# Gated tiles on ScalarE, the selection in one piece on VectorE, the second gather in other banks, W2 in quarters

## The chip, the cores and the metric

One Trainium2 chip, one core. A core has TensorE (matmuls into eight PSUM banks), VectorE, ScalarE, GpSimd and SyncE, and 16 DMA engines that all queues share. The metric is the time of one launch in device microseconds; lower is better.

## The reference

The input x is (16, 1024, 512), 16 batches of 1024 tokens. Two residual steps follow each other: a gated cross attention over 64 context tokens a batch (the first half of the kernel, which the change does not touch), and a gated expert step, which it does. The expert step, cut to what matters:

```python
x = x + jnp.tanh(g_ffn[0]) * ffn(_layernorm(x))
# ffn: DM, NEXPERTS, SETS, ESIZE = 512, 32, 4, 32  -> 128 experts of width 32
grouped = x.reshape(b, s // g, g, d)                            # groups of g = 32 tokens
logits = einsum('bntd,des->bntes', grouped, Wc) + bc + tie
perm = (logits == max(logits, over the 32 tokens of a group))   # each expert picks a token of each group
permuted = einsum('bntd,bntes->bnesd', grouped, perm)           # gather
inner = relu(einsum('bnesd,esdf->bnesf', permuted, W1) + b1)
result_permuted = einsum('bnesf,esdf->bnesd', inner, W2) + b2
result = einsum('bnesd,bntes->bntd', result_permuted, perm)     # scatter back
```

W1 and W2 are 8 MB each in float32; every batch needs both whole.

## The kernel before, in words

`experts` writes one instruction stream for each engine by hand; semaphores (`Mark`, with `at(i, k)` for the k-th event of batch i) order them. The loop runs over i = 0 to 16: step i works on batch i, finishes batch i-1, and prepares batch i+1. On TensorE a step is:

1. `gather(i, n)`, n = 0 to 7: selected tokens of one quarter of D (c) and one half of the tokens (h) are multiplied by the one-hot `sel` into banks 4 to 7. ScalarE and VectorE share the copy out to `gat` (`copy`, L1259 and L1302). Each gather waits until both copies of the one before are done. `bias(i)` (L1371) starts the accumulators, banks 0 to 3, and stands behind gather 0. `inner(i, p)` (L1388) multiplies `gat` by one eighth of W1 and runs two gathers behind.
2. `scatter(i-1, t)` (L1426), t = 0 to 7, into banks 4 to 7 in turn; `finish(i-1, t)` (L1306, VectorE) multiplies the tile by the gate into SBUF, and GpSimd adds it to `out` in DRAM with an accumulating DMA (`add_to_out`, L1221). A scatter from the fifth on waits for the finish four back.
3. `outer(i, u)`, u = 0 to 7 (L1406 and L1411): eight parts of W2, in two bank groups in turn. `rest(i, u)` copies each out, one half on ScalarE (L1269), one on VectorE (L1316). `outer(u)` waits for the copies of `outer(u-2)`, and `outer(1)` for the last finish, since it uses banks 4 to 7.
4. `chosen_T(i+1, h)` (L216) transposes the next batch's one-hot matrix, `chosen` (ScalarE, L221) copies it into `sel`.

VectorE also turns `res` in place (`swap`, L1296, eight a step, one behind each gather copy), and makes the selection of the next batch, `pick` (L199, L207, L210: add bias, maximum of the group, compare) for two halves h. The logits of a half are first scaled on GpSimd (`scaled`, L191), and the tokens of the next batch are normalised there (`normed`, L184).

Where the weights lie: three eighths of W1 and five of W2 (u = 0 to 4) stay in SBUF. The others come anew each batch. W1's come in quarters of 256 KB from SyncE (L1159, L1167). W2's u = 5, 6, 7 (`W2_MOVED`) come into the space of `gat` as three DMAs of 1 MB from ScalarE (`load_second`, L1147), once `inner` has read `gat` for the last time. SyncE also loads the next batch's eight token tiles (`load_x`, L174, 256 KB each) and per half two transfers of 256 KB for the logits (L178 and L179). Token tiles 4 to 7 take the places of gated tiles 0 to 3: they wait until the accumulating DMAs of those have landed, and each waits for the one two before it.

`dynamic_dma_scratch_size` is the space in SBUF for the descriptors of GpSimd's DMAs; here 1024.

The landings of W2's parts are waited for in `outer`:

```python
if u in W2_MOVED:
    e.wait_ge(d_room[u].sem, d_room[u].at(i, d_room[u].per - 1))
```

Of the kernel before, what the change touches and what calls it, by code (L numbers as in the profile page):

```python
# [17 lines left out]
P = 128  # L18
# [3 lines left out]
E, G = 128, 32  # L22
# [1023 lines left out]
def experts(nc, top, ps, kept, d_kept, consts, ident, gate_f, xin, ring, d_ring, route, m_b2s, w1_dram, w2_dram, out):  # L1046
# [7 lines left out]
    with st:  # L1054
# [16 lines left out]
        d_room = {u: mark(f"room{u}", 1, 16) for u in W2_MOVED}  # L1071
# [9 lines left out]
        bank = lambda u: u % 2 * 4  # L1081
        middle = y.rearrange("p n d -> p (n d)")
# [39 lines left out]
        def gathered(n, g):  # L1122

            return (gat[:, n // 2 % 2, :].rearrange("p (e h g t) -> p h e g t", h=2, g=GT, t=TH)[:, n % 2, :, g],
                    ps[:, 4:8, :].rearrange("p g (t e) -> p e g t", t=TH)[:, :, g])
# [18 lines left out]
        def load_second(e, i, u):  # L1144

            e.wait_ge(m_w1.sem, m_w1.at(i, 7 if u == W2_MOVED[2] else 5))
            e.dma_start(second(i, u), w2_dram[u].rearrange("p (k d) -> p k d", d=D)).then_inc(d_room[u].sem, 16)  # L1147
# [5 lines left out]
        def sync(e):  # L1153
# [33 lines left out]
            for i in range(B + 1):  # L1187
# [6 lines left out]
                for h in range(2):  # L1194
                    if live(i + 1):
                        load_x(i + 1, 2 * h)
                        load_x(i + 1, 2 * h + 1)
                        if h:
                            e.wait_ge(m_w1.sem, m_w1.at(i, 6))
                        else:  # L1200
                            e.wait_ge(m_gap.sem, m_gap.at(i, 2 * C - 1))
                        route.load_logits(e, i + 1, h)
                if live(i + 1):
                    for t in range(NY, NT):
                        load_x(i + 1, t)
# [11 lines left out]
        def gpsimd(e):  # L1217
# [5 lines left out]
            for i in range(B):  # L1223
# [4 lines left out]
                for t in (0, 1):  # L1228
                    if live(i - 1):
                        add_to_out(i - 1, t)  # L1230
# [3 lines left out]
                for t in (2, 3):  # L1234
                    if live(i - 1):
                        add_to_out(i - 1, t)
                if live(i + 1):
                    route.scaled(e, i + 1, 1)
# [15 lines left out]
        def scalar(e):  # L1254
# [10 lines left out]

            def rest(i, u):
                e.wait_ge(m_w2.sem, m_w2.at(i, u))
                o, v = pair_of(u, 0)
                e.activation(o, v, ACT.Copy).then_inc(m_evA.sem, 1)  # L1269

            for i in range(B):
                if live(i):
                    for n in range(2 * C):
                        copy(i, n)
                    for p in (2 * C - 2, 2 * C - 1):
                        for j in range(4):
                            hidden(i, j, p)
                        load_second(e, i, W2_MOVED[p % 2])
                    load_second(e, i, W2_MOVED[2])
                for u in range(8):  # L1280
                    rest(i, u)
# [9 lines left out]
        def vector(e):  # L1291
# [12 lines left out]
            def finish(i, t):  # L1304
                e.wait_ge(m_sc.sem, m_sc.at(i, t))
                e.tensor_scalar(tile_of(t), ps[:, 4 + t % 4, :], gate_f[:], None, ALU.mult).then_inc(m_fin.sem, 1)  # L1306

# [10 lines left out]
            for i in range(B + 1):  # L1318
# [8 lines left out]
                for t in range(NT):  # L1327
                    if live(i - 1) and i < B:
                        finish(i - 1, t)
                    if live(i + 1) and t in (3, 4, 5):  # L1330
                        pick(i + 1, 0, t - 3)
                for u in range(8):
                    if live(i):
                        rest(i, u)
                    if live(i + 1) and u in (1, 3, 5):
                        pick(i + 1, 1, u // 2)
# [6 lines left out]
        def tensor(e):  # L1343
# [4 lines left out]
            def gather(i, n):  # L1348

                c, h = piece(i, n) // 2, n % 2  # L1350
                if n:
                    e.wait_ge(m_gaA.sem, m_gaA.at(i, n - 1))
                    e.wait_ge(m_gaV.sem, m_gaV.at(i, n - 1))
                elif i:
# [4 lines left out]
                for t in range(TH):  # L1359
                    for g in range(GT):  # L1360
                        r = slice(g * G, (g + 1) * G)
                        last = e.matmul(ps[:, 4 + g, t * E:(t + 1) * E], xn[r, h * TH + t, c * P:(c + 1) * P], sel[r, h * TH + t, :],  # L1362
# [3 lines left out]
            def bias(i):  # L1366

                e.wait_ge(m_sel.sem, m_sel.at(i, 1))
# [74 lines left out]
            for i in range(B + 1):  # L1443
                if live(i):
                    for n in range(2 * C + 2):
                        if n < 2 * C:
                            gather(i, n)
                        if n == 0:
# [64 lines left out]
```

## Time and profile before

| | |
|---|---|
| median of 3 runs | 1838.23 us (1836.72 to 1841.11) |
| the profiled execution | 1830.52 us, of it the span of the trace 1828.7 us |
| busy share of the span | TensorE 90%, VectorE 76%, GpSimd 47%, ScalarE 37% |
| first scatter of the expert stage | 971.5 us |
| 14 periods of it, scatter to scatter | 806.5 us, 57.6 us each |
| mean granted clock of TensorE | 0.971 |

The profile is one execution. Times in the trace count from the start of the span. An expert period is told here from one scatter (first L1426) to the next; the rows are mostly of the one from 1429.75 to 1489.24 us.

### The profile page before, as it was taken

Reading aid. Unit: us, or ns where it says so; the run is one execution under the profiler, and the core shown is the slowest. Engines: PE = TensorE matmul, PEld = TensorE weight load, DVE = VectorE, ACT = ScalarE, POOL = GpSimd, SP = SyncE. Lnnn points to the kernel's source line nnn. Section 1 sums busy time; section 2 is a strip of 40 time slices with the busy share of each in tenths; the row PEclk is TensorE's granted clock in tenths of the full one; section 3 lists DMA queues with packets and bytes.
Section 4 is the critical chain, followed back from the end, with each engine's and each line's share of the span. In section 5 each row is a group of like instructions: output and inputs, shape, how many; then the busy total and the mean of one; then the engine's idle time right before and its main releaser. Section 6 shows DMA issues by size and latency. Waiting matters only on the chain.

```text
span 1828.7 us, 51599 instructions
## 1 busy us (share of the span) xinstructions
PE 1638.1 (90%) x22488; PEld 1146.1 (63%) x22488; DVE 1381.1 (76%) x1976; ACT 681.6 (37%) x875; POOL 859.7 (47%) x1016
## 2 busy tenths in 40 slices
PE   7899999999999999999888888878888888888985
PEld 4677777777777777776654566445654456544662
DVE  6677777777777777777467887778877787877786
ACT  3533233233233333232244444444444434444442
POOL 3466777777777777776223312233122322233122
PEclk9899999999999999999889999999999999999998
DMA  7534545344454445444458766778767876778666
GB/s 274 158 113 142 170 151 172 119 163 146 140 177 143 144 141 172 143 166 150 142 179 220 223 209 173 199 219 227 208 160 199 228 208 173 188 209 229 198 165 164
DMA packets 160146, 324.79 MB, mean 178 GB/s; under 512 B 21041, under 2 KB 31025, under 8 KB 152369
## 3 DMA queue, kind: packets, MB, share of 16 engines
q1 hardware_dynamic: 135728, 239.68, 41.1%
q0 software_dynamic: 17280, 31.46, 10.4%
q10 hardware_dynamic: 6912, 50.33, 7.1%
q8 instruction: 179, 2.93, 0.8%
q14 instruction: 47, 0.38, 0.1%
HBM read 242.71 MB, written 78.71 MB: 176 GB/s over the span
## 4 chain that ended last, share of the span: by engine, by line
PE 69%; DVE 13%; issue 9%; ACT 4%; POOL 2%; DMA 2%; SPq 1%; POOLq 0%; ACTq 0%; DVEq 0%
PE ps L1388 14%; PE ps L877 10%; PE ps L924 10%; PE ps L1362 8%; PE ps L1411 6%; PE ps L937 5%; PE ps L1426 3%; PE ps L892 3%; PE ps L1406 3%; PE ps L950 2%; DVE mx L675 2%; DVE xin L1306 2%; PE ps L911 2%; ACT res L1269 1%; DVE lg L679 1%
## 5 line engine op out<-in xcount | busy, mean ns | idle before, releaser
L184 POOL TENSOR_SCALAR xin<-xin,r_all,nb_all 128x512 f32<-128x512 f32 x128 | 109.8, 996 | 403.9 <-DMA xin<-out 403.8
L1296 DVE STREAM_TRANSPOSE res<-res 128x2048 f32<-128x2048 f32 x128 | 292.0, 2295 | 0.1
L1259 ACT ACTIVATE gat<-ps 128x1536 f32<-128x1536 f32 (+1 forms) x128 | 172.2, 1345 | 220.7 <-PE ps L1362 220.7
L1221 POOL DMA_DIRECT2D out<-xin x120 | 115.8, 1018 | 212.9 <-issue 143.7
L1269 ACT ACTIVATE res<-ps 128x1024 f32<-128x1024 f32 x128 | 131.2, 1025 | 226.0 <-PE ps L1411 226.0
L877 PE MATMUL ps<-xTh,qh 128*128 128x512 f32 x512 | 209.9, 410 | 5.4 <-DVE qs L692 1.9
L877 PE MATMUL ps<-xTh,ql 128*128 128x512 f32 x512 | 201.2, 393 | 0.0
L877 PE MATMUL ps<-xTl,qh 128*128 128x512 f32 x512 | 200.7, 392 | 0.0
L1362 PE MATMUL ps<-sel,xin 32*128 32x128 f32 x4096 | 159.7, 292 | 41.6 <-DVE gat L1302 22.9
L1316 DVE COPY res<-ps 128x1024 f32<-128x1024 f32 x128 | 153.8, 1217 | 42.6 <-PE ps L1411 41.6
L532 POOL TENSOR_TENSOR qc<-qc,qs 128x512 f32<-128x512 f32 x64 | 82.8, 1294 | 209.1 <-DVE qs L692 209.1
L1362 PEld LDWEIGHTS ps<-sel,xin 32*128 32x128 f32 x4096 | 134.8, 194 | 67.2 <-ACT gat L1259 46.5
L1302 DVE COPY gat<-ps 128x512 f32<-128x512 f32 (+1 forms) x128 | 104.1, 813 | 90.0 <-PE ps L1362 89.6
L519 POOL TENSOR_TENSOR xTl<-xT,xTh 128x512 fp32r<-128x512 f32 x128 | 160.5, 1284 | 11.1 <-ACT xTh L575 11.1
L924 PE MATMUL ps<-vw,pTh 128*128 128x512 f32 x512 | 165.4, 404 | 0.0
L707 DVE TENSOR_TENSOR xin<-ps,xin 128x512 f32<-128x512 f32 x128 | 88.3, 690 | 69.5 <-PE ps L924 69.5
L1406 PEld LDWEIGHTS ps<-b2s,rowk 32*128 32x128 f32 x512 | 28.0, 196 | 179.8 <-issue 114.9
L691 DVE TENSOR_TENSOR qc<-ps,cos 128x512 f32<-128x512 f32 x128 | 86.8, 678 | 59.7 <-PE ps L877 59.7
L1306 DVE TENSOR_SCALAR xin<-ps,gate_f 128x512 f32<-128x512 f32 x120 | 88.2, 744 | 47.4 <-PE ps L1426 42.0
L924 PEld LDWEIGHTS ps<-vw,pTh 128*128 128x128 f32 x512 | 94.7, 190 | 45.6 <-issue 25.2
L1406 PE MATMUL ps<-b2s,rowk 32*128 32x512 f32 x512 | 70.3, 533 | 59.0 <-issue 28.4
L877 PEld LDWEIGHTS ps<-xTh,qh 128*128 128x128 f32 x512 | 96.9, 189 | 35.8 <-DVE qs L692 18.4
(156 smaller groups left out, 3372.2 us busy)
## 6 DMA issues: line engine op xcount, KB each, us to landing
gat<-in_W ACTq DMA_DIRECT2D x48, 1024.0 KB, 9.1
xT<-in_xT SPq DMA_DIRECT2D x32, 1024.0 KB, 6.0
xin<-in_x SPq DMA_DIRECT2D x64, 512.0 KB, 3.8
out<-xin SPq DMA_DIRECT2D x64, 512.0 KB, 3.7
xin<-out SPq DMA_DIRECT2D x128, 256.0 KB, 4.7
xin<-in_W SPq DMA_DIRECT2D x128, 256.0 KB, 3.4
out<-xin POOLq DMA_DIRECT2D x120, 256.0 KB, 7.0
xT<-in_W SPq DMA_DIRECT2D x68, 256.0 KB, 4.2
```

Source lines behind the costliest of these rows:

```text
L519: e.tensor_tensor(xTl[:, c, :], xT[:, c, :], xTh[:, c, :].bitcast(F32), ALU.subtract).then_inc(m_lo.sem, 1)
L877: last = e.matmul(ps[:, 2 + n % 2, :], a[:, c, n * DH:(n + 1) * DH], b[:, c, :], start=(k == 0), stop=(k == len(parts) - 1))
L924: last = e.matmul(ps[:, 5 + t % 2, :], a[:, t // 2, column:column + P], vw[:, u // 2 % 2, k, p, :], start=(m == 0), stop=(m == len(parts) ...
L1221: e.dma_start(batch(out, b, t, 1)[:, 0], tile_of(t), accum_op=ALU.add).then_inc(d_ys[t].sem, 16)
L1259: e.activation(o, v, ACT.Copy).then_inc(m_gaA.sem, 1)
L1269: e.activation(o, v, ACT.Copy).then_inc(m_evA.sem, 1)
L1296: e.transpose(v, v).then_inc(m_tr.sem, 1)
L1306: e.tensor_scalar(tile_of(t), ps[:, 4 + t % 4, :], gate_f[:], None, ALU.mult).then_inc(m_fin.sem, 1)
L1316: e.tensor_copy(o, v).then_inc(m_evV.sem, 1)
L1362: last = e.matmul(ps[:, 4 + g, t * E:(t + 1) * E], xn[r, h * TH + t, c * P:(c + 1) * P], sel[r, h * TH + t, :], start=True, stop=True)
L1388: last = e.matmul(ps[a * 64:(a + 1) * 64, q // 8, q % 8 * 64:(q % 8 + 1) * 64], first(i, p)[:, (e0 % 64) * F:(e0 % 64 + 2) * F], gat[:, c ...
L1406: e.matmul(ps[:, bank(u) + j, :], rowk[r, u // 2, :], b2s[r, u % 2, :], start=True, stop=False, skip_group_check=True)
```

## The change

- `finish` moves from VectorE to ScalarE, as an activation with a scale.
- `pick`: all six steps of the next batch stand together ahead of `rest(i, 0)` on VectorE (for i = 0 ahead of `rest(0, 5)`), where three were put between the finishes and three between the rests.
- GpSimd: `scaled(i+1, 1)` stands right behind `scaled(i+1, 0)`, ahead of all eight `add_to_out`. SyncE loads the logits of the second half before token tiles 2 and 3.
- `gather(i, 1)` goes to banks 0 to 3 and doesn't wait for the copies of gather 0; `gather(i, 2)` waits for those. `bias` moves behind gather 2 and waits for the copies of gather 1.
- W2's three parts come in quarters (12 DMAs of 256 KB): u = 5 beside the ReLUs of the last piece, 6 and 7 one quarter behind each finish.
- The descriptor space doubles to 2048.

```diff
-        d_room = {u: mark(f"room{u}", 1, 16) for u in W2_MOVED}
+        d_room = {u: mark(f"room{u}", QUARTERS, 16) for u in W2_MOVED}
...
+        front = lambda n: 0 if n == 1 else 4
...
-                    ps[:, 4:8, :].rearrange("p g (t e) -> p e g t", t=TH)[:, :, g])
+                    ps[:, front(n):front(n) + 4, :].rearrange("p g (t e) -> p e g t", t=TH)[:, :, g])
...
-        def load_second(e, i, u):
+        def load_second(e, i, u, c):
 
             e.wait_ge(m_w1.sem, m_w1.at(i, 7 if u == W2_MOVED[2] else 5))
-            e.dma_start(second(i, u), w2_dram[u].rearrange("p (k d) -> p k d", d=D)).then_inc(d_room[u].sem, 16)
+            e.dma_start(quarter(second(i, u).rearrange("p k d -> p (k d)"), c), quarter(w2_dram[u], c)).then_inc(d_room[u].sem, 16)
...
-                for h in range(2):
-                    if live(i + 1):
-                        load_x(i + 1, 2 * h)
-                        load_x(i + 1, 2 * h + 1)
-                        if h:
-                            e.wait_ge(m_w1.sem, m_w1.at(i, 6))
-                        else:
-                            e.wait_ge(m_gap.sem, m_gap.at(i, 2 * C - 1))
-                        route.load_logits(e, i + 1, h)
                 if live(i + 1):
-                    for t in range(NY, NT):
+                    load_x(i + 1, 0)
+                    load_x(i + 1, 1)
+                    e.wait_ge(m_gap.sem, m_gap.at(i, 2 * C - 1))
+                    route.load_logits(e, i + 1, 0)
+                    e.wait_ge(m_w1.sem, m_w1.at(i, 6))
+                    route.load_logits(e, i + 1, 1)
+                    for t in range(2, NT):
                         load_x(i + 1, t)
...
                     route.scaled(e, i + 1, 0)
-                for t in (0, 1):
+                    route.scaled(e, i + 1, 1)
+                for t in range(NY):
                     if live(i - 1):
                         add_to_out(i - 1, t)
                 if live(i + 1):
                     route.normed(e, i + 1, 2)
                     route.normed(e, i + 1, 3)
-                for t in (2, 3):
-                    if live(i - 1):
-                        add_to_out(i - 1, t)
-                if live(i + 1):
-                    route.scaled(e, i + 1, 1)
...
+            def finish(i, t):
+                e.wait_ge(m_sc.sem, m_sc.at(i, t))
+                e.activation(tile_of(t), ps[:, 4 + t % 4, :], ACT.Copy, scale=gate_f[:]).then_inc(m_fin.sem, 1)
+
...
                             hidden(i, j, p)
-                        load_second(e, i, W2_MOVED[p % 2])
-                    load_second(e, i, W2_MOVED[2])
+                            if p % 2:
+                                load_second(e, i, W2_MOVED[0], j)
+                for t in range(NT):
+                    if live(i - 1) and i < B:
+                        finish(i - 1, t)
+                    if live(i):
+                        load_second(e, i, W2_MOVED[1 + t // QUARTERS], t % QUARTERS)
...
-                for t in range(NT):
-                    if live(i - 1) and i < B:
-                        finish(i - 1, t)
-                    if live(i + 1) and t in (3, 4, 5):
-                        pick(i + 1, 0, t - 3)
                 for u in range(8):
+                    if live(i + 1) and u == (0 if i else 5):
+                        for h in range(2):
+                            for step in range(3):
+                                pick(i + 1, h, step)
                     if live(i):
                         rest(i, u)
-                    if live(i + 1) and u in (1, 3, 5):
-                        pick(i + 1, 1, u // 2)
...
-                if n:
-                    e.wait_ge(m_gaA.sem, m_gaA.at(i, n - 1))
-                    e.wait_ge(m_gaV.sem, m_gaV.at(i, n - 1))
-                elif i:
+                if n >= 2:
+                    k = 0 if n == 2 else n - 1
+                    e.wait_ge(m_gaA.sem, m_gaA.at(i, k))
+                    e.wait_ge(m_gaV.sem, m_gaV.at(i, k))
+                elif n == 0 and i:
                     copied(e, i - 1, 7)
...
-                e.wait_ge(m_sel.sem, m_sel.at(i, 1))
+                e.wait_ge(m_gaA.sem, m_gaA.at(i, 1))
+                e.wait_ge(m_gaV.sem, m_gaV.at(i, 1))
...
-                        if n == 0:
+                        if n == 2:
                             bias(i)
...
-    nc = bacc.Bacc("TRN2", target_bir_lowering=False, num_devices=1, dynamic_dma_scratch_size=1024)
+    nc = bacc.Bacc("TRN2", target_bir_lowering=False, num_devices=1, dynamic_dma_scratch_size=2048)
```

## Rows read from the trace of the kernel before

**Rows 1.** The page: busy us of each engine, share of the span, instructions.
```profile
PE 1638.1 (90%) x22488; PEld 1146.1 (63%) x22488; DVE 1381.1 (76%) x1976; ACT 681.6 (37%) x875; POOL 859.7 (47%) x1016
```

**Rows 2.** Periods: length, busy PE, PEld, DVE, ACT, POOL, granted clock, DMA share, GB/s.
```profile
1429.75:1489.24 59.49, 50.77 (x1140) 31.95 (x1137) 44.93 (x38) 24.40 (x26) 16.32 (x18) 0.91 0.72 194
...
971.50:1778.00 806.50, 680.78 (x15907) 433.00 (x15905) 631.46 (x532) 346.58 (x365) 229.85 (x250) 0.96 0.73 202
```

**Rows 3.** Timeline, TensorE, one period: start, length, line, idle before and releaser.
```profile
1429.75 7.09 PE L1426 MATMUL ps<-res,selT 128*32 128x512 f32 x64
1436.77 0.50 PE L1406 MATMUL ps<-b2s,rowk 32*128 32x512 f32 x4
...
1439.82 0.51 PE L1406 MATMUL ps<-b2s,rowk 32*128 32x512 f32 x4 [1.48 <-DVE xin L1306]
...
1447.16 0.80 PE L1406 MATMUL ps<-b2s,rowk 32*128 32x512 f32 x4 [2.67 <-issue]
...
1460.77 1.17 PE L1362 MATMUL ps<-sel,xin 32*128 32x128 f32 x32 [0.52 <-ACT gat L1259]
1463.38 1.92 PE L1362 MATMUL ps<-sel,xin 32*128 32x128 f32 x32 [1.43 <-DVE gat L1302]
1465.23 2.88 PE L1388 MATMUL ps<-gat,xT 128*64 128x64 f32 x64
```

**Rows 4.** Timeline, TensorE, step 0: outer 4, transposes, gather 0, bias.
```profile
933.58 0.50 PE L1406 MATMUL ps<-b2s,rowk 32*128 32x512 f32 x4
...
940.00 1.06 PE L216 MATMUL ps<-ident,selT 128*128 128x128 f32 x8
941.95 1.17 PE L1362 MATMUL ps<-sel,xin 32*128 32x128 f32 x32 [0.89 <-ACT sel L221]
942.91 1.07 PE L1371 MATMUL ps<-ident,b1r 32*128 32x512 f32 x8
```

**Rows 5.** Timeline, VectorE: the pick that waits, a gather copy.
```profile
1445.17 0.75 DVE L199 SCALAR_TENSOR_TENSOR gat<-gat,bcol,tie 128x512 f32<-128x512 f32 x1 [2.36 <-POOL gat L191]
...
1462.00 1.23 DVE L1302 COPY gat<-ps 128x1024 f32<-128x1024 f32 x1 [1.33 <-PE ps L1362]
```

**Rows 6.** Groups by shape, ScalarE, 14 periods: the copy out of one bank.
```profile
L221 ACT ACTIVATE sel<-ps 128x512 f32<-128x512 f32 x28 | 15.3, 595 | 12.0 <-PE ps L216 12.0
```

**Rows 7.** Timeline, GpSimd: the adds and what stands between them.
```profile
1432.05 1.78 POOL L1221 DMA_DIRECT2D out<-xin  x2 [2.38 <-DVE xin L1306]
...
1442.58 0.89 POOL L1221 DMA_DIRECT2D out<-xin  x1 [6.35 <-issue]
1443.14 2.00 POOL L191 TENSOR_TENSOR gat<-gat 128x512 f32<-128x512 f32 x1
...
1451.62 3.29 POOL L184 TENSOR_SCALAR xin<-xin,r_all,nb_all 128x512 f32<-128x512 f32 x4
```

**Rows 8.** Stretches of 2 us, columns as in rows 2: the first and the last of 12.
```profile
1430.00:1432.00 2.00, 2.00 (x24) 0.58 (x20) 1.00 (x2) 1.93 (x4) 0.00 (x0) 1.00 1.02 382
...
1452.00:1454.00 2.00, 2.00 (x52) 0.53 (x36) 1.24 (x2) 1.02 (x1) 2.00 (x4) 0.66 1.10 196
```

**Rows 9.** DMA, 1438 to 1440 us: packets, MB, share of 16 engines.
```profile
q10 hardware_dynamic: 64, 0.49, 62.5%
q0 software_dynamic: 68, 0.14, 36.9%
```

**Rows 10.** DMA, 1430 to 1442 us: ScalarE's queue, and W2's time to landing.
```profile
q10 hardware_dynamic: 401, 2.89, 60.0%
...
gat<-in_W ACTq DMA_DIRECT2D x2, 1024.0 KB, 10.4
```

**Rows 11.** DMA, 1442 to 1455 us: GpSimd's queue and SyncE's.
```profile
q0 software_dynamic: 842, 1.52, 69.8%
q1 hardware_dynamic: 576, 1.05, 27.9%
```

**Rows 12.** DMA, 1456 to 1478 us: SyncE's queue with quarters of W1 alone.
```profile
q1 hardware_dynamic: 1377, 2.52, 36.4%
```

More of the change, by code:

```diff
@@ L1277, in scalar @@
                             hidden(i, j, p)
-                        load_second(e, i, W2_MOVED[p % 2])
-                    load_second(e, i, W2_MOVED[2])
+                            if p % 2:
[5 more added lines that the diff above has]
+                        load_second(e, i, W2_MOVED[1 + t // QUARTERS], t % QUARTERS)
                 for u in range(8):
-                    rest(i, u)
+                    if live(i):
+                        rest(i, u)
                 if live(i + 1):
@@ L1302, in copy @@
                 e.tensor_copy(o, v).then_inc(m_gaV.sem, 1)
-            def finish(i, t):
-                e.wait_ge(m_sc.sem, m_sc.at(i, t))
-                e.tensor_scalar(tile_of(t), ps[:, 4 + t % 4, :], gate_f[:], None, ALU.mult).then_inc(m_fin.sem, 1)
             def pick(i, h, step):
@@ L1361, in gather @@
                         r = slice(g * G, (g + 1) * G)
-                        last = e.matmul(ps[:, 4 + g, t * E:(t + 1) * E], xn[r, h * TH + t, c * P:(c + 1) * P], sel[r, h * TH + t, :],
+                        last = e.matmul(ps[:, front(n) + g, t * E:(t + 1) * E], xn[r, h * TH + t, c * P:(c + 1) * P], sel[r, h * TH + t, :],
                                         start=True, stop=True)
```

## The prediction

> **What bounds the kernel now.** The page first: TensorE is busy 90% of the span and no other engine comes near [rows 1]. The attention half is not touched, so the next view is the busy time of each stretch from scatter to scatter. The 14 expert periods take 806.5 us, 57.6 each, at a granted clock of 0.96; the one I read closely takes 59.49 at 0.91 [rows 2]. A period is mostly TensorE's chain, so its timeline says what can go. The waits there [rows 3]: 1.48 us before outer 1 (VectorE's last finish), 2.67 before outer 4, 0.52 and 1.43 before the second and third gather (copies). The 2.67 has no releaser named. VectorE's timeline gives it: a pick waits 2.36 us for GpSimd's scaled logits [rows 5], and the copies out of the outers stand behind it. GpSimd's timeline says why that is late: the fourth accumulating DMA is held up for 6.35 us, and only then comes the scaling, 2.00 us [rows 7]. TensorE also drops to its lower level after these waits (gather 2 takes 1.92 us, where gather 1 took 1.17 [rows 3]).
>
> Last I read the DMA share in stretches of 2 us. It is 1.02 in the first from 1430 and 1.10 in the last to 1454, and 1.037 in the mean of these 12 [rows 8]: **the 16 DMA engines are full during the whole scatter and outer phase.** The mean share over the period, 0.72 [rows 2], hides that.
>
> **The change part by part.** *Gated tiles on ScalarE.* A copy of 128x512 from PSUM costs ScalarE 0.595 us [rows 6]. A scatter comes each 0.88 us (7.02/8, [rows 3]) and ScalarE has only its ReLUs before, so the last finish ends less than 1 us after the last scatter, inside outer 0. The 1.48 us goes. A cover is needed for the DMA issues that now stand between: twelve, where there were three, one behind each finish, about 0.4 us each by an estimate, on the sequencer beside the running activation. Bound: 0 to 0.4 us of them on the path; I take 0.
>
> *Selection in one piece, scaling ahead of the adds.* GpSimd's second scaling no longer stands behind the add that waited. It now waits for its logits with all eight adds behind it: the first add moves from 1432.05 to about 1434 if the logits land in 5 us, as it is an SP load placed ahead of token tiles 2 and 3. The picks then fit between the swaps and rest 0. The 2.67 us goes, and with it the rests that held up the transposes.
>
> *Outer phase without these waits.* Four outers take 940.00 - 933.58 = 6.42 us [rows 4], so 1.605 each. From 1436.77 [rows 3] eight end at 1449.6. Gather 0 came 1.95 us after them in the step without a wait [rows 4]: 1451.6.
>
> *Second gather in other banks.* Before, gather 2 came 2 x 2.6 us after gather 0 (the pitch of 1460.77 to 1463.38 [rows 3]). Now gather 1 follows at once, gather 2 comes after 2.6, and bias must wait for VectorE's second copy, 1.23 us [rows 5], then take 1.07 [rows 4]: inner 0 starts 4.9 us behind gather 0, not 6.3 at full clock. That is 1.4 us less, and another 0.75 where gather 2 ran at the lower level.
>
> *What stays.* From inner 0 (1465.23) to the next scatter (1489.24) 24.0 us; about 0.75 of it is the lower clock again, so 23.25. **If no transfer is late** the period is 1451.6 + 4.9 + 23.25 - 1429.75 = 50.0 us.
>
> *Is one late?* The work of the DMA engines behind 1430, in us of all 16:
> - eight adds: 1.52 MB took 69.8% of 13 us [rows 11], so 1.56 for 0.262 MB; 12.5.
> - token tiles 4 to 7: 1.05 MB took 27.9% of 13 us [rows 11]; 3.6.
> - W2 in three parts of 1 MB: 2.89 MB took 60.0% of 12 us [rows 10], so 3.15 MB take 7.85. In quarters it has the form of W1's: 2.52 MB took 36.4% of 22 us [rows 12], 0.83 a quarter, **10.0** for the twelve.
> - the rest of the second logits and of tiles 2 and 3: some 2.5 before, and I take 1.5 now (tiles 2 and 3 start later, W2 too).
>
> Before: 26.4 us of work, over 1.037 that is 25.5, an end at 1455.5. The trace agrees: full to 1454, and tile 7 is normalised from 1451.62 on, some 3.3 us [rows 7]. After: 27.6, an end at 1456.6. So the engines are busy as long as before, and the question is only who comes last.
>
> Here the quarters weigh more than by their 2.2 us. From 1438 to 1440 ScalarE's queue and GpSimd's both had work: 64 packets against 68, but 0.49 MB against 0.14 [rows 9]. They are served **packet for packet**, and a packet of a 1 MB load carries four times as much as one of a quarter. In the kernel before, W2 had all landed by about 1442 (10.4 us [rows 10]), eleven us before outer 7 needed it. In quarters W2 has 12 x 128 packets against 8 x 128 of the adds and 4 x 128 of the tiles. Some three quarters pass before the first add, at 1434; the nine others take turns with eight adds and four tiles, and the last quarter is then behind nearly everything: 1456.6, less one add of 1.5 that may come after it, and some 1 us until it has landed: 1456.1. Outer 7 would be due at 1436.77 + 7 x 1.605 = 1448.0. It **waits about 8 us**.
>
> The Trainium skill, "DMA: Bandwidth & Descriptors", section "Rules for kernel authors", speaks against the quarters in another way: it wants 1 MiB or more a transfer. Its fit (2.0 us plus the bytes over 436 GB/s) gives 4.4 us for 1 MB and 2.6 for a quarter, 31 us for twelve one behind the other, an end past 1461. The trace does not bear that out as engine time, since W1's quarters took 0.83 us each [rows 12].
>
> The sum: outer 7 at 1456.1, and after 8 us of idling TensorE is at its lower level (0.80 us against 0.50 for the same four matmuls after a wait of 2.67 [rows 3]): 1.6 + 1.0 us. Then 1.95 + 0.4 to gather 0 at 1461.05, 4.9 to inner 0, 23.25 to the next scatter: 1489.2. Period 59.4, against 57.6: some 1.7 us more, times 14 is 24. At the ends: step 0 gains 1.4 at its gathers and loses 2.5, as six picks (some 4 us) stand ahead of rest 5; the last step has no tiles to load, and its 12.5 + 10.0 us over 1.037 still put outer 7 some 4 us later. Together 5. Predicted: 1838.2 + 24 + 5 = **1867 us**; on the profiled execution, which is 7.7 below the median, 1859.5. The unknowns of this sum: a quarter may cost only 0.75, the share reach 1.08 and the clock cost nothing (1825), or all land 2 us later with more at the lower level (1900).
>
> **The rivals.**
> 1. *W2 stays ahead of the adds* (faster). The mechanism: quarters issued before and between the adds are served in the order of issue, and the queue of adds yields. It decides where W2's last quarter lands, from 1448 down it costs nothing. Then tile 7 is the late thing, at 1455, normalised by 1456. Gather 1 waits for it, and 1.2 + 1.3 + 1.1 later, at 1459.6, comes inner 0: period 53.1, 4.5 less, 1776 us. For it: W2 filled 60% of the engines' time while adds waited [rows 10]. Against it: that was with packets of 8 KB, and one for one [rows 9].
> 2. *No transfer is late*, the shares overlap more than they add up. Period 50.0, 1733 us. Against it: 12 stretches in a row at a share of one [rows 8].
> 3. *GpSimd is the late one.* The second logits land as slowly as W2 did (10.4 us, [rows 10]), all adds begin at 1440, tile 7 is normalised at 1458, and W2, less disturbed, is early. Period about 58, 1846 us.
> 4. *A quarter costs the engines 1.2 us*, between 0.83 and an add's 1.56: 4.4 us more a period, 1929 us. That is where the skill's fit points. Against it: [rows 12].
>
> **How the numbers follow.** The forecast's own case 0.55 (0.04 of it faster, 0.05 the same), rival 1 0.25, rival 2 0.08, rival 3 0.08 (0.01 of it the same), rival 4 0.04. What can be told from no change is about 0.2%, some 4 us. Slower 0.46 + 0.07 + 0.04 = 0.57, same 0.06, faster 0.37. The own range of the forecast's case is 1825 to 1900. For 8 in 10 it must reach to rival 1: 1762 to 1898 leaves out rivals 2 and 4 and the outer part of rival 1.
>
> **What would show it.** Right: the waits before outer 1 and outer 4 gone; gather 1 directly behind gather 0, inner 0 about 4.9 behind it; the first add near 1434 in this period's time, and the fourth right behind it; a wait of 5 to 9 us with no engine as releaser before outer 7, perhaps a small one before outer 6; W2's quarters with times to landing that grow from 3 to over 12 us; a DMA share of one until the end of that wait. Wrong: eight outers in one piece and the wait at gather 1 (rival 1), or nowhere (rival 2); VectorE's picks waiting for GpSimd past 1438 (rival 3).

## The result, and the profile after

The changed kernel takes 1820.83 us (median of 9 runs, 1812.23 to 1824.39) against 1838.23 (9 runs): a ratio of 0.9907, 95% interval 0.9884 to 0.9930. **It is 17 us faster; 29 us slower were forecast.** The profiled execution took 1812.23 us, with a span of 1810.4; it is the fastest of the nine. Times are medians over all executions; experiments 13 and 15 each had one far above the rest (3935 and 2021 us), which the ratios leave out.

The stretches of the expert stage first. The columns are length, busy time of PE, PEld, DVE, ACT and POOL, granted clock, DMA share and GB/s.

```profile
904.00:972.86 68.86, 58.03 (x1550) 43.57 (x1544) 40.44 (x34) 31.82 (x33) 11.55 (x13) 0.95 0.54 174
972.86:1759.24 786.38, 695.19 (x15908) 438.35 (x15904) 539.65 (x420) 414.88 (x477) 234.73 (x250) 0.95 0.75 207
```

The 14 periods take 786.4 us, not 806.5 [rows 2]: 56.17 each, where the forecast had 59.4. Before them 1.4 us are lost, behind them 0.5. VectorE is busy 540 us of it, not 631.

TensorE in one period (start, length, line, what it waited for):

```profile
1084.92 3.64 PE L1425 MATMUL ps<-res,selT 128*32 128x512 f32 x32
1088.82 3.65 PE L1425 MATMUL ps<-res,selT 128*32 128x512 f32 x32 [0.26 <-ACT xin L1262]
1092.40 0.51 PE L1405 MATMUL ps<-b2s,rowk 32*128 32x512 f32 x4
...
1108.53 0.80 PE L1405 MATMUL ps<-b2s,rowk 32*128 32x512 f32 x4 [3.96 <-DMA gat<-in_W]
...
1113.21 2.07 PE L1360 MATMUL ps<-sel,xin 32*128 32x128 f32 x64 [0.57 <-ACT sel L221]
1115.82 1.17 PE L1360 MATMUL ps<-sel,xin 32*128 32x128 f32 x32 [0.54 <-DVE gat L1306]
1116.95 1.14 PE L1370 MATMUL ps<-ident,b1r 32*128 32x512 f32 x8
1118.02 2.09 PE L1387 MATMUL ps<-gat,xT 128*64 128x64 f32 x64
```

The waits of [rows 3] before outer 1 and outer 4 are gone. Gathers 0 and 1 are one piece of 64 matmuls, and inner 0 is 4.8 us behind gather 0 in this period (6.0 in the mean, since in some periods a gather waits for a token tile). One wait is new: outer 7, at the lower clock after it, for a part of W2. TensorE's waits over the 14 periods (us in total, times, longest):

```profile
PE ps L1405 <- DMA gat<-in_W: 44.8, 13, 4.6
PE ps L1387 <- issue: 12.1, 20, 1.2
PE ps L1360 <- POOL xin L184: 11.5, 6, 4.9
```

So 3.2 us a period for W2, where the forecast had 8, and 0.8 for token tiles that GpSimd normalises, where it had nothing.

GpSimd in the same period:

```profile
1087.21 1.60 POOL L191 TENSOR_TENSOR gat<-gat 128x512 f32<-128x512 f32 x1 [2.09 <-DMA gat<-r_scratch]
1089.13 3.57 POOL L1219 DMA_DIRECT2D out<-xin  x4 [0.32 <-ACT xin L1262]
...
1092.94 4.52 POOL L1219 DMA_DIRECT2D out<-xin  x3
1097.84 0.87 POOL L1219 DMA_DIRECT2D out<-xin  x1 [0.37 <-issue]
1105.57 0.77 POOL L184 TENSOR_SCALAR xin<-xin,r_all,nb_all 128x512 f32<-128x512 f32 x1 [6.87 <-DMA xin<-out]
...
1112.74 0.77 POOL L184 TENSOR_SCALAR xin<-xin,r_all,nb_all 128x512 f32<-128x512 f32 x1 [0.31 <-DMA xin<-out]
```

The adds go out in one run, where the fourth waited 6.35 us [rows 7]. Tile 7 is normalised 28.6 us behind the scatter's start (28.8 in the mean over the periods, 25.7 before the change).

### The profile page after: what moved, and what is told of

Read it like the earlier page. It is cut to its first block, busy times and chain, and to the rows that moved or that the text cites. A ratio compares the mean times of both kernels' runs of the same rounds, so it can differ in the third digit from the quotient of the medians.

```text
span 1810.4 us, 51743 instructions
## 1 busy us (share of the span) xinstructions
PE 1654.5 (91%) x22488; PEld 1152.1 (64%) x22488; DVE 1283.6 (71%) x1856; ACT 754.5 (42%) x995; POOL 866.3 (48%) x1016
## 4 chain that ended last, share of the span: by engine, by line
PE 59%; DVE 12%; DMA 10%; issue 9%; POOL 5%; ACT 3%; ACTq 1%; SPq 1%; DVEq 0%; POOLq 0%
PE ps L1387 14%; PE ps L877 10%; PE ps L924 10%; DMA gat<-in_W 8%; PE ps L1360 7%; PE ps L937 5%; PE ps L892 3%; PE ps L950 2%; DVE mx L675 2%; PE ps L1425 2%; POOL out L1219 2%; POOL xin L184 2%; PE ps L911 2%; PE ps L1410 1%; DVE lg L679 1%
## 5 line engine op out<-in xcount | busy, mean ns | idle before, releaser
L184 POOL TENSOR_SCALAR xin<-xin,r_all,nb_all 128x512 f32<-128x512 f32 x128 | 122.0, 1129 | 502.0 <-DMA xin<-out 501.8
L1360 PE MATMUL ps<-sel,xin 32*128 32x128 f32 x4096 | 155.1, 290 | 26.9 <-POOL xin L184 11.5
L1219 POOL DMA_DIRECT2D out<-xin x120 | 129.1, 1817 | 49.9 <-ACT xin L1262 33.5
L691 DVE TENSOR_TENSOR qc<-ps,cos 128x512 f32<-128x512 f32 x128 | 86.9, 679 | 59.4 <-PE ps L877 59.3
L592 ACT ACTIVATE lx<-ps 128x512 f32<-128x512 f32 x32 | 19.1, 598 | 246.1 <-PE ps L937 246.1
```

What stands on the lines that cost most here:

```text
L184: e.tensor_scalar(self.xn[:, t, :], self.xn[:, t, :], self.r[:, i, t:t + 1], self.nb[:, i, t:t + 1], ALU.mult, ALU.add).then_inc(self.m_xn ...
L1219: e.dma_start(batch(out, b, t, 1)[:, 0], tile_of(t), accum_op=ALU.add).then_inc(d_ys[t].sem, 16)
L1360: last = e.matmul(ps[:, front(n) + g, t * E:(t + 1) * E], xn[r, h * TH + t, c * P:(c + 1) * P], sel[r, h * TH + t, :], start=True, stop=True)
```

## The experiments

All are compared with runs of the kernel before on the same chip (1830 to 1835 us). "Changed" stands for the kernel above. Where a mean over periods is given, it is from the 14 periods of the one profiled execution, which can lie some 10 us from the median of its kernel (1812.23 against 1820.83 for the changed kernel, 1823.54 against 1813.05 in experiment 5).

**1. W2 whole.** In the changed kernel:

```diff
-                            if p % 2:
-                                load_second(e, i, W2_MOVED[0], j)
+                            if p % 2 and j == 0:
+                                load_second(e, i, W2_MOVED[0])
...
-                        load_second(e, i, W2_MOVED[1 + t // QUARTERS], t % QUARTERS)
+                    if live(i) and t % QUARTERS == 0:
+                        load_second(e, i, W2_MOVED[1 + t // QUARTERS])
```

> The changed kernel with W2's three moved parts as whole DMAs of 1 MB (u = 5 behind the first ReLU of the last piece, u = 6 behind finish 0, u = 7 behind finish 4), all else as changed. Theory 1, the queues take turns packet for packet: in quarters W2 gave a packet of 2 KB for each packet of the adds (144 against 144 in 2 us); with 8 KB packets its last part lands 5 us or more sooner, the wait before outer 7 (3.7 us in the mean) goes, and the adds and behind them token tiles 4 to 7 come later: a wait of 1 to 3 us at gather 0 or 1 instead. Time 1785 to 1805 us. Theory 2, the DMA engines have a fixed amount of work and whoever comes last costs the same: the wait only moves from outer 7 to the gathers, time within 5 us of the changed kernel (1816 to 1826).

Measured: 1797.13 us, ratio 0.9814 (0.9769 to 0.9860). The wait for W2 is gone from TensorE's list, and one at the gathers has grown:

```profile
PE ps L1360 <- POOL xin L184: 51.0, 14, 4.8
PE ps L1360 <- ACT sel L221: 12.8, 14, 0.9
```

The wait moved from W2 (3.2 us a period, now 0.1 before outer 7) to the tiles (0.8, now 3.6), as theory 1 has it, and the time is in its range. But that move alone gains nothing: all of TensorE's waits are 5.9 us a period, where they were 6.3. What W2 takes of the DMA engines, over the 14 periods (packets, MB, share), is different, in the changed kernel and then in this one:

```profile
q10 hardware_dynamic: 24192, 44.05, 17.2%
```

```profile
q10 hardware_dynamic: 6048, 44.04, 14.7%
```

That is 9.7 us a period (17.2% of 56.17) against 8.1 (14.7% of 55.29), and tile 7 is normalised 1.5 us sooner (27.3, not 28.8). 1.5 us in 14 periods would be 21 of the 24 us gained. So the shorter work of whole parts is at least as good an explanation of the gain as who gets the turns. No run here separates the two, nor the third difference: the last part of W2 is issued 4.8 us behind the scatter's start, the last quarter 7.6.

**2. W2's quarters sooner.** `load_second(e, i, W2_MOVED[p % 2], j)` beside every ReLU, u = 7 behind finishes 0 to 3.

> The changed kernel with its quarters issued sooner: u = 5 beside the ReLUs of piece 6, u = 6 beside those of piece 7, u = 7 behind finishes 0 to 3. The DMA share between the pieces was 0.4 to 0.6 there, so 2 to 3 us of W2's work move ahead of the adds. Theory 1 (the head start over the adds sets when W2's last quarter lands): it lands some 2.5 us sooner, the wait before outer 7 falls to about 1 us, 1.5 to 2.5 us a period less, 1785 to 1800 us. Theory 2 (the end of all DMA work is what counts): the second logits land later behind the quarters, the adds begin later, token tiles are late; same time as the changed kernel.

Measured: 1822.31 us, ratio 0.9943 (0.9920 to 0.9965). A miss for theory 1, and what theory 2 had written down: the adds begin later, the tiles are late, the time is that of the changed kernel. W2's wait did fall, to 0.9 us a period, but the gathers wait 3.6 for tiles and the scatter 0.9 for ScalarE:

```profile
PE ps L1359 <- POOL xin L184: 50.3, 13, 5.0
PE ps L1404 <- DMA gat<-in_W: 12.9, 9, 4.6
PE ps L1424 <- ACT xin L1262: 12.2, 10, 2.6
```

The first add goes out 6.7 us behind the scatter's start, not 4.4. What W2 wins the tiles lose.

**3. and 4. Without the bank change**, with quarters and with W2 whole: `front = lambda n: 4`, each gather waits for the copies of the one before, bias behind gather 0.

> The changed kernel with the second gather back in banks 4 to 7, waiting for the copies of gather 0, and the bias behind gather 0, as in the kernel before. Prices the bank change alone. Both theories: inner 0 comes 6.3 us behind gather 0, not 4.8, and nothing else is late: 1.4 us a period, 15 periods, 20 us more: 1841 us. If token tiles 4 to 7 bound the gathers in many periods, gather 1 comes late enough anyway and it costs less, some 12 us.

> W2 whole and the second gather in banks 4 to 7: what is left of the change is the gated tiles on ScalarE, the selection in one piece, the scaling ahead of the adds, and the descriptor space. Theory 1: token tiles 4 to 7 come late, but gather 1 is 2.6 us behind gather 0 here, which hides most of it: 1800 to 1815. Theory 2: 1838 to 1845.

Measured: 1834.19 us (ratio 1.0008, 0.9983 to 1.0034) and 1819.46 (0.9935, 0.9909 to 0.9961). The bank change is worth 13 us with quarters and 22 us with W2 whole. Without it the changed kernel is no faster than before: the other parts together bring nothing. The first is near the 12 us that were expected if the tiles bound the gathers; the second is 4.5 us above its nearer range.

**5. and 6. One part alone in the kernel before**: the quarters (issued where the whole parts were), the banks.

```diff
-                        load_second(e, i, W2_MOVED[p % 2])
-                    load_second(e, i, W2_MOVED[2])
+                        for c in range(QUARTERS):
+                            load_second(e, i, W2_MOVED[p % 2], c)
+                    for c in range(QUARTERS):
+                        load_second(e, i, W2_MOVED[2], c)
```

> The kernel before with one part of the change: W2's three moved parts in quarters, issued where the whole ones were. Its adds begin at the same time but three of them wait on the descriptor space, and outer 7 comes 24.5 us behind the scatter's start, not 18. Theory 1 (turns packet for packet; W2's last quarter lands 23 to 25 us behind the scatter's start): hardly a wait at outer 7, but the second logits land sooner (they share turns with smaller packets) and the token tiles too: within 6 us of before, 1830 to 1842. Theory 2 (a quarter costs by itself, some 24 us in the changed kernel): 1850 to 1862.

> The kernel before with the bank change alone (second gather in banks 0 to 3, bias behind gather 2). Inner 0 comes 1.4 us sooner behind gather 0, if token tiles 4 to 7 are there: they are normalised at 1454.9 in the period read, gather 1 would stand at 1459.3, so it is not held up. Both theories 15 to 16 periods x 1.4 = 22 us less, 1812 us. If the whole cycle is held by the DMA engines, which start and end it, the gain is smaller, under 10 us.

Measured: 1813.05 us (0.9885, 0.9837 to 0.9933) and 1810.22 (0.9867, 0.9827 to 0.9907). The banks give what was expected. The quarters are a surprise: **they gain 20 us here and lose 24 in the changed kernel.** The second logits' last transfer lands after 6.6 us (median over the periods), not 10.6, so scaling and picks come sooner; the wait before outer 4 falls. Both forecasts for the quarters were missed. In the changed kernel both transfers of the second logits are issued ahead of W2's first quarter (1083.16 and 1083.52 against 1085.04), so that there the quarters have little to give; that this is all of the difference is argued, not shown.

**7. Small adds.** The accumulating DMAs move columns 0 to 127 only, so three quarters of the expert step's sum are left out of the output.

```diff
-                e.dma_start(batch(out, b, t, 1)[:, 0], tile_of(t), accum_op=ALU.add)
+                e.dma_start(batch(out, b, t, 1)[:, 0, 0:P], tile_of(t)[:, 0:P], accum_op=ALU.add)
```

> The changed kernel with the accumulating DMAs moving only 128 of 512 columns: it leaves out three quarters of the expert step's addition to the output (batches 0 to 14). All waits and issues stay. The DMA engines' work in the window falls by up to 8 us of 27. Theory 1 and 2: the wait before outer 7 and those at the gathers go and the period is the one worked out for no late transfer, 50 to 51 us: 1810 - 14 x 5.5 = 1735 to 1750 us. If TensorE waits as before, it was not the DMA engines' work, and the sum without a late transfer was wrong.

Measured: 1732.31 us, ratio 0.9452 (0.9406 to 0.9498). The periods of this kernel:

```profile
974.62:1678.62 704.00, 662.12 (x15909) 424.70 (x15905) 536.67 (x420) 413.54 (x477) 232.42 (x250) 1.00 0.68 200
```

704.0 / 14 is 50.3 us, where the prediction had 50.0 for "no transfer late", and 1733 us. The time is 3 us below the range expected. With less for the DMA engines to do, the wait for W2 is gone (0.02 us a period) and that for tiles is 0.4. Of the 5.9 us a period by which this kernel is shorter than the changed one, 3.6 are these two waits and 2.4 are TensorE's own work, 47.3 us for 49.7, at a granted clock of 1.00 for 0.95. The 2.8 us of waits that are left are others.

**8. Later adds.** The normalising of tiles 2 and 3 ahead of the first add.

> The changed kernel with the normalising of token tiles 2 and 3 ahead of the first add on GpSimd, so that adds start 2 to 3 us later. Theory 1 (what W2's last quarter has ahead of it is the number of adds that have begun; the first add's packets come 4 us behind its issue): the wait before outer 7 falls by 1 to 2 us and the gathers wait more for tiles 4 to 7, in sum the same or up to 1.5 us a period more: 1820 to 1842 us. If the start of the adds does not matter for W2, the wait before outer 7 stays at 3.2 us in the mean and the gathers' is 2 us longer: 1840 or more.

Measured: 1824.78 us (0.9950, 0.9924 to 0.9975). The first add goes out at 7.0 us, not 4.4; W2's wait falls from 3.2 to 0.4 us a period, that for tiles grows from 0.8 to 4.9 (over the 14 periods):

```profile
PE ps L1360 <- POOL xin L184: 68.5, 16, 5.3
PE ps L1405 <- DMA gat<-in_W: 5.0, 4, 2.2
```

When the first packet of an add moves, 1397 of W2's 1728 packets have passed here in the mean, and 914 in the changed kernel. So **the start of the adds decides which of the two waits**, as theory 1 has it. The two waits together are 1.3 us a period longer; in the time it is 4 us, not clear of noise.

**9. Banks and quarters in the kernel before**, nothing else.

> The kernel before with both the bank change and the quarters, without the moved finishes, the selection in one piece, the early scaling and the larger descriptor space. The two parts alone gave 1810 and 1813 against 1833. If their gains add up (the quarters let the logits land sooner, outer 4 waits less; the banks give 1.4 us a period): 1790 to 1798. If the DMA engines' end holds the cycle, the wait before outer 7 (0.9 us a period with the quarters alone) grows by what the banks save: 1805 to 1815, and then the remaining part of the change, not the quarters alone, is what made the changed kernel lose.

Measured: **1783.27 us, ratio 0.9735 (0.9711 to 0.9758)**: faster than the changed kernel by 37 us. That is 50 us gained, more than the 20 and 23 of the two parts alone, and more than either forecast had. TensorE's waits over its 14 periods:

```profile
PE ps L1411 <- DVE xin L1309: 20.1, 14, 1.5
PE ps L1393 <- issue: 16.4, 18, 2.0
PE ps L1411 <- DMA gat<-in_W: 12.6, 6, 2.7
```

That for token tiles is 0.05 us a period. It keeps the waits that the change removed, and its first add goes out 2.3 us behind the scatter's start, its tile 7 is normalised at 25.8.

**10. to 12. Three more on the changed kernel:** W2 whole with u = 5 issued ahead of the ReLUs and the picks of step 0 spread; the same with u = 7 in quarters; the descriptor space back at 1024.

> The changed kernel with W2 whole, u = 5 issued as soon as gat is free of piece 5 (ahead of the ReLUs, some 5 us before the last piece ends), u = 6 behind finish 0 and u = 7 behind finish 4, and the picks of step 0 spread between its rests (it had a wait of 3.9 us there). 2.6 us of W2's work move to where the DMA share is 0.4. Theory 1 with a conserved amount of work in the window: tiles 4 to 7 land up to 2.6 us sooner, the wait at the gathers (3.6 us in the mean with W2 whole) falls to 1 to 2 us: 1765 to 1782 with 3 us from step 0. Against it: the logits share turns with W2 as in the other kernel with early W2, the adds start later, same as W2 whole: 1790 to 1797.

> As the one before, but u = 7, the part needed last, in quarters behind finishes 4 to 7. Theory 1: W2's last part gives up turns to the adds where it has time to (needed 18 us behind the scatter's start, whole it landed before 15); tiles 4 to 7 land about 1 us sooner, outer 7 waits 0 to 1 us: within 5 us of the one before, either side. If quarters only cost: 5 to 12 us more.

> The changed kernel with the descriptor space back at 1024. Three adds go out, the fourth waits until the first has landed (10 us), and the tiles 2 and 3 with it. Theory 1: fewer adds in turn with W2, so W2's last quarter lands 3 to 5 us sooner and outer 7 hardly waits, but tiles 4 to 7 land as late or later: gathers wait 3 to 5 us. 1815 to 1835. If the larger space did nothing, the two waits are as in the changed kernel.

Measured: 1787.14 us (0.9745, 0.9718 to 0.9772), 1787.31 (0.9748, 0.9720 to 0.9775) and 1805.10 (0.9833, 0.9795 to 0.9872). The early u = 5 and the spread picks together gained 10 us on experiment 1, not 15 to 32, and no run separates the two: the gathers still wait 3.2 us a period for tiles, and the adds went out 1.5 us later than in experiment 1 (6.0, not 4.5). The second is within 5 us of the first, as expected. The third was 10 us below its range: the larger descriptor space cost 16 us. With the small one tile 7 is there 1.1 us sooner (27.7, not 28.8) and the wait for W2 is 1.3 us, not 3.2; that for tiles is 2.3, not 0.8, since the outers end sooner. That the cost comes from six and more adds in flight, which take turns from both, fits this but is argued.

**13. and 14. One more part each on the kernel of experiment 9:** the space at 2048; the finishes on ScalarE (behind all twelve issues of W2).

> The kernel before with banks and quarters (1783 us), plus the larger descriptor space alone. The fourth add and the second scaling no longer wait (5 to 6 us), so the wait before outer 4 goes (1.5 us a period); against that six or more adds are in turn with W2's quarters and with tiles 4 to 7. Theory A (the number of adds in flight costs, as in the changed kernel): wait before outer 7 grows from 0.9 to 3 us: 1795 to 1810. Theory B (the space cost only together with the late start of the adds): 1770 to 1783.

> The kernel before with banks and quarters, plus the gated tiles on ScalarE alone (picks of the first half ahead of rest 0). The 1.44 us before outer 1 go; the first finish comes behind eight ReLUs, some 1 us later than on VectorE, so adds and tiles 4 to 7 land 1 us later, which no gather waits for yet (0.05 us). Theory A: the DMA engines' window ends at the same time, and outer 7 waits for W2 what outer 1 no longer waits: 1780 to 1786. Theory B: a gain of 1 us a period: 1765 to 1775. Theory C, the finishes on ScalarE are what costs: 1790 or more.

Measured: 1822.24 us (0.9944, 0.9918 to 0.9970) and 1819.59 (0.9941, 0.9913 to 0.9970). Each alone undoes most of the gain. The first is 12 us above its highest range; the second is where theory C had it (1790 or more), but for a reason that no theory named. With the larger space VectorE's first pick takes 5.2 us in most periods. The same instruction in the two kernels, first with the small space, then with the large one:

```profile
L199 DVE SCALAR_TENSOR_TENSOR sel<-sel,bcol,tie x16: 743/1800/1824, 879.4 to 1689.6; 128x512 f32<-128x512 f32 x16
```

```profile
L199 DVE SCALAR_TENSOR_TENSOR sel<-sel,bcol,tie x16: 743/5190/5332, 880.9 to 1727.3; 128x512 f32<-128x512 f32 x16
```

(minimum, median and maximum in ns). GpSimd works beside it in both; in the second without a pause, as the fourth add no longer waits. In 9 of the 14 periods with the large space the pick took 5.2 us or a little more, and GpSimd's scaling began 1.9 to 2.1 us after the pick did and ended before it; in the other five it took 1.4 to 1.8, and was done before the scaling began. The pick stands between the finishes, so outer 1 waits 3.9 us in the mean, not 1.4. With the finishes on ScalarE behind the issues:

```profile
1144.84 4.62 ACTq L1148 DMA_DIRECT2D gat<-in_W  x5
1149.52 2.42 ACT L1269 ACTIVATE xin<-ps,gate_f 128x512 f32<-128x512 f32 x4 [4.41 <-issue]
```

Five issues took 4.62 us of ScalarE's sequencer, and the scatter waited 2.8 us a period for the finishes. The first add went out at 6.8 us, where 1 us later than 2.3 was expected.

**15. and 16. The second scaling behind the second add**, in the changed kernel with the small space and with the large one:

```diff
-                    route.scaled(e, i + 1, 1)
                 for t in range(NY):
                     if live(i - 1):
                         add_to_out(i - 1, t)
+                    if live(i + 1) and t == 1:
+                        route.scaled(e, i + 1, 1)
```

> The changed kernel with the small descriptor space (1805 us), and the second scaling behind the second add, not ahead of the first. Adds 0 and 1 start up to 2 us sooner (as soon as finish 0 is there), so tiles 4 to 7 land sooner. Theory A (the adds' late start is the rest of the cost): the gathers' wait of 2.3 us falls to about 1, 1780 to 1795. Against it: the second scaling comes 2 us later, picks end just ahead of rest 0. If the start of the adds does not matter: 1800 to 1810.

> The same with the large space, the changed kernel otherwise (1821 us). Theory A: adds start up to 2 us sooner, which takes W2's head start away and gives it to the tiles: the wait before outer 7 grows by about 1 us, that at the gathers (0.8) goes: 1815 to 1825. Theory B, the early start helps here too: 1800 to 1812.

Measured: 1803.62 us (0.9851, 0.9806 to 0.9896) and 1822.68 (0.9954, 0.9927 to 0.9981), beside 1805.10 and 1820.83. No effect. The first add went out 0.3 to 0.5 us sooner only: in all 15 steps it waits for ScalarE's first finish, not for the scaling. With the large space the two waits moved in the direction that theory A had, W2's from 3.2 to 3.7 us a period and the tiles' from 0.8 to 0.4.

**17. and 18. The parts of 13 and 14 without their accidents:** the finishes on ScalarE between the issues of W2, as the change has them; the space at 2048 with the picks behind the finishes.

> The kernel before with banks and quarters, the finishes on ScalarE and W2's issues between them as in the change (u = 5 beside the ReLUs of the last piece, then one quarter behind each finish); small descriptor space, scaling behind the fourth add. The wait before outer 1 (1.44) goes and the scatter waits under 0.3. W2 is issued 2 to 5 us later than in the 1783 kernel, so outer 7 waits more than its 0.9. Theory A (the DMA engines' window ends when it ends): 1775 to 1790. If the later issue of W2 is what the change paid: outer 7 waits 3 us, 1795 to 1805, near the changed kernel with the small space (1805).

> The kernel before with banks, quarters and the large descriptor space, with the three picks of the first half behind all finishes on VectorE. Theory: the 5.2 us pick was VectorE and GpSimd in each other's way; behind the finishes it no longer holds them, outer 1 waits about 1 us and rest 0 2 us more at most, so 30 us of the space's cost go: 1785 to 1800, the rest being W2's wait before outer 7 (1.6). If the number of adds in flight is the cost, 1810 or more with a wait of 3 us before outer 7.

Measured: 1827.13 us (0.9973, 0.9945 to 1.0002) and 1799.85 (0.9831, 0.9792 to 0.9869). The first is a miss of 37 us, and neither theory had it. The wait is before outer 4: VectorE's copies stand behind a pick, that behind the second scaling, and that behind the fourth add, which waits for the first to land. Now that the scatter and outer 1 don't wait, the outers arrive sooner, and the adds later (4.1 us, not 2.3). TensorE's timeline of the kernel with the finishes between the issues, at outer 4's first matmuls:

```profile
1157.49 0.80 PE L1411 MATMUL ps<-b2s,rowk 32*128 32x512 f32 x4 [4.58 <-issue]
```

and VectorE's in the same period, at the pick ahead of those copies:

```profile
1155.51 0.75 DVE L199 SCALAR_TENSOR_TENSOR gat<-gat,bcol,tie 128x512 f32<-128x512 f32 x1 [4.27 <-POOL gat L191]
```

So with the finishes on ScalarE the second scaling has to come ahead of the fourth add: 1805 us with it ahead of all adds and 1804 behind the second (experiments 12 and 15), 1827 behind the fourth. These kernels differ in the places of the picks and in SyncE's order too, so the 22 us are not the scaling's alone for certain. With the finishes on VectorE both can be left. The second is at the edge of its range, and the pick takes 1.8 us again: of the 39 us that the space cost, 22 went with the pick's place (what that place gives with the small space wasn't tried). Of the 17 that are left the wait for W2, 2.2 us a period where it was 0.9, makes 17 as well; the space costs 16 in the changed kernel.

## Why the prediction was wrong, by its steps

**What bounds the kernel** was right: the full DMA engines. Experiment 7 shows it, and comes within 0.3 us a period of the sum for "no transfer late".

**Finishes, picks, outers, gather 1:** right in time. The waits before outer 1 and 4 are gone, the outers run at 1.6 us, and gather 0 to inner 0 is 4.8 us for 4.9 where no tile is late. The first add is issued 4.2 us behind the scatter's start in this period, as forecast.

**Packet for packet** was right, and the trace after shows it better than [rows 9]. From 1096.92 to 1098.92 us (packets, MB, share):

```profile
q0 software_dynamic: 144, 0.26, 70.9%
q10 hardware_dynamic: 144, 0.26, 39.7%
```

**The step that failed is "some three quarters pass before the first add, at 1434", and "the last quarter is then behind nearly everything".** I let the adds take turns from the moment of their issue. The first add here went out at 1089.13. In the first two stretches of 2 us behind the scatter's start, up to 1088.92, 6 + 129 = 135 of W2's 1728 packets had passed: one quarter and not three, as its first issue is at 1085.04 and no longer 2.4 us ahead of the scatter. That slip would have made outer 7 later still. But GpSimd's queue moves its first packet only between 1093.0 and 1093.5:

```profile
q0 software_dynamic: 1, 0.00, 2.2%
```

That is some 4.3 us after the issue, and until then W2 has the engines nearly alone. In the stretch from 1090.92 to 1092.92:

```profile
q10 hardware_dynamic: 394, 0.72, 104.6%
```

With the 282 of the stretch before it, 135 + 282 + 394 = 811 of W2's 1728 packets have passed by its end, and some more until the first add is under way: nearly six quarters, not three. The other six take turns with six adds, not eight, and tiles 6 and 7 come after them. In the mean over the periods 239 packets (1.7 quarters) have passed when the first add is issued, and 914 (6.3 quarters) when its first packet moves, 4.3 us later. Outer 7 could start 23.6 us behind the scatter's start here (22.5 in the mean), not 26.35, and its wait was 3.2 us, not 8. The same delay was to be read before the change: the adds of 1432.05 [rows 7] moved nothing until 1436.4, with 97.8% of the engines' time W2's from 1434 to 1436. I had read the stretch from 1438 on, and not the one in which the adds should have begun. Experiment 8 is the test of what the start of the adds does: with it 2.7 us later, W2's wait is 2.8 us shorter.

**Terms of the sum** were off by less. A quarter costs 16.4% of 56.94 us over 12, 0.78 us for 0.83; an add 20.1% over 8, 1.43 for 1.56; together 1.7 us of 27.6 too much. The 24 us in the sum are 25 by its own numbers (59.4 less 57.6, 14 times). The fit that the prediction takes from the Trainium skill, "DMA: Bandwidth & Descriptors", stands there in the section "Anatomy of one DMA — SWDGE (gpsimd) path", for DMAs issued from GpSimd, and W2's come from ScalarE; no term of the sum used it. The mean DMA share of the 12 stretches of 2 us behind the scatter's start is 1.04, as forecast.

**The cost of tile 7** was left out: I took it for early because W2 was to be late. It is normalised at 28.8 us behind the scatter's start in the mean, before the change at 25.7; that gave the 0.8 us a period at the gathers. So of the forecast 59.4 us a period, W2 takes 4.8 less and the tiles 0.8 more (with 0.2 at the scatter): 55.6, and 56.2 was measured. The 0.6 between them isn't accounted for.

**The ends:** six picks ahead of rest 5 in step 0 cost 3.9 us, where I had 2.5 (outer 7 there waits for VectorE's copy of outer 5, which stands behind them). The last step waited 1.7 us, not 4.

**Rival 1** was nearer than the forecast in its sign, not in its mechanism: W2 was not ahead. With W2 whole (experiment 1) W2 was ahead, and it gave 1797 us, where the rival had 1776: the gathers wait 3.6 us for tiles.

**In the size of the parts**, what no step of mine had: two of the six parts carry everything, the other four together cost. From the kernel before with banks and quarters (1783) to the whole change are 37 us, of them some 16 for the descriptor space (experiment 12, and 18 with 17 in the other arrangement). The rest, 22 us between 1783 and 1805, is with the finishes on ScalarE and the orders on GpSimd and SyncE that go with them. With the small space in both, the first add goes out at 4.6 us, not 2.3, the fourth has landed at 21.0, not 19.0, and tile 7 comes at 27.7, not 25.8. That fits those 22 us, but moving the scaling (experiment 15) did not bring the adds forward, so that this alone is the cause is argued, not shown. Finishes on ScalarE ahead of its last ReLUs weren't tried, nor W2 whole with the small space.

## What to carry to other kernels

Where the DMA engines are full, a wait removed on the compute side is paid by whichever transfer now comes last, so list the transfers that share the stretch, in packets and in the order of their first packet, before counting any gain. The size of a transfer is then also a priority: a large one gets ahead, small ones let another queue through. Small ones have a price too, here 9.7 us of the engines a period for 8.1. The same cut into quarters gained 20 us in one order and lost 24 in another. Try the parts of a change one by one: the fastest complete kernel here is the kernel before with two of them.

## What was not expected of the hardware

- An accumulating DMA of 256 KB from GpSimd moved its first packet some 4 us after its issue began: 4.4 us before the change and 4.3 after, in the mean of 14 periods (1432.05 to 1436.4 and 1089.13 to 1093.4 in those told above). It is not a constant: in experiments 11 and 14 it was 2.4 us in the mean, and 1.5 at the least. What sets it stays open.
- VectorE's scalar_tensor_tensor of 128x512 between SBUF tiles took 0.75 us alone and 1.8 beside GpSimd's normalising and adds (experiment 9), or its scaling and adds (18). In experiment 13 it took 5.2 us in 9 of 14 periods: there GpSimd went from normalising through two adds to the scaling without a pause, and the scaling ran before the pick was done. In the other five it took 1.4 to 1.8. What decides between the two stays open.
- Issues of quarters from ScalarE in a row took 0.4 us at first; one of the later ones took 1.65, and the five from 1144.84 on 4.62 together, with the finishes behind them.
- W2's 3.15 MB a period took 9.7 us of the 16 engines in quarters and 8.1 whole, in the mean of 14 periods (17.2% of 56.17, 14.7% of 55.29): a fifth more in packets of 2 KB than in packets of 8 KB.
